# A two-layer relational graph network on one core: loads, x transposes and degree products of the front stage in another order

## The reference, cut to what matters

```python
# layer 0: degree of each node, counting the self loop; 1/sqrt(deg) on both ends of an edge
deg = segment_sum(ones, col, n); dinv = rsqrt(deg)
out = segment_sum((x @ W0)[row] * (dinv[row] * dinv[col])[:, None], col, n) + b0
x = layernorm(x + out)
# layer 1, twice (4 heads, then 1): per relation r
xr = einsum('nd,rdf->rnf', x, W); oi = xr[etype, dst]; oj = xr[etype, src]
alpha = leaky_relu(oi @ q + oj @ k); softmax over the edges with one dst
out = segment_sum(a * oj, dst, n) + b        # elu after the first
x = layernorm(x + layer1)
```

## Time and profile before

| | us |
|---|---|
| median of 3 runs | 1607.62 |
| lowest, highest | 1606.1, 1608.44 |
| the profiled execution | 1607.62 |
| its span | 1605.8 |

### The profile page before, as it was taken

The page is one execution under the profiler, slowest core; times in us unless marked ns, Lnnn a source line. Parts: engine busy times, 40 slices in busy tenths (PEclk is TensorE's granted clock), DMA queues, the critical chain, the costliest instruction groups (busy, mean ns, idle before and its releaser), DMA issues. The chain is left out here.

```text
span 1605.8 us, 23070 instructions
## 1 busy us (share of the span) xinstructions
PE 1396.8 (87%) x7239; PEld 1101.0 (69%) x7239; DVE 1135.7 (71%) x2394; ACT 401.6 (25%) x1013; POOL 385.4 (24%) x389
## 2 busy tenths in 40 slices
PE   6899978888888779999599999849998996999991
PEld 5566624554454479999599999828998993555550
DVE  9888887887776179995598888671554334666767
ACT  2222212233233111112244444352221210000003
POOL 1000000000000000000677777200000007777740
PEclk9799989999899889999799999959998997999996
DMA  6344301232232396662899998506664559999973
GB/s 223 138 158 157 137 3 52 81 99 71 80 104 70 120 328 204 206 178 76 311 328 318 321 328 300 135 4 202 189 191 135 189 163 312 323 322 318 319 221 96
DMA packets 105814, 301.51 MB, mean 188 GB/s; under 512 B 17677, under 2 KB 47183, under 8 KB 105663
## 3 DMA queue, kind: packets, MB, share of 16 engines
q1 hardware_dynamic: 77551, 160.68, 31.2%
q0 software_dynamic: 28160, 139.52, 25.6%
HBM read 245.31 MB, written 57.18 MB: 188 GB/s over the span
## 5 line engine op out<-in xcount | busy, mean ns | idle before, releaser
L1278 DVE CUSTOM_DVE_ANT_0 fl_early<-fl_masks,fl_gap 125x1250 bf16<-125x1250 f32 x120 | 166.8, 1465 | 23.6 <-DMA fl_masks<-fl_d_k 19.3
L815 PE MATMUL fr_ps<-fr_col_hot,fr_row_hot 125*128 x516 | 122.0, 368 | 50.0 <-DVE fr_col_hot L553 44.6
L1171 POOL DMA_INDIRECT xH<-fl_d_xr,edge_row x88 | 96.1, 1092 | 252.6 <-DMA fl_d_xr<-fl_xs 221.4
L1171 POOL DMA_INDIRECT xH<-sl_d_xr,edge_row x88 | 86.8, 987 | 270.9 <-DMA sl_d_xr<-sl_xs 240.8
L860 PE MATMUL fr_ps<-fr_h,fr_shared 125*125 125x384 f32 x400 | 142.1, 505 | 1.7 <-DVE fr_shared L581 1.7
L1549 PE MATMUL sl_ps<-xH,sl_hot 128*125 128x386 f32 x352 | 118.6, 495 | 17.6 <-DVE sl_hot L1352 17.5
L1509 PE MATMUL fl_ps<-fl_wH,xH 128*125 128x384 f32 x360 | 122.5, 340 | 9.6 <-ACT fl_xs L1192 9.6
L1228 ACT ACTIVATE fl_masks<-fl_plain,fl_ex 128x125 f32<-128x125 f32 x352 | 106.8, 385 | 93.8 <-PE fl_ps L1545 70.3
L1509 PE MATMUL sl_ps<-sl_wH,xH 128*125 128x384 f32 x360 | 124.7, 346 | 5.9 <-DVE sl_wL L1268 5.9
L1545 PE MATMUL fl_ps<-xH,fl_masks 128*125 128x194 f32 x704 | 121.5, 333 | 9.4 <-DVE fl_masks L1345 9.2
L1545 PEld LDWEIGHTS fl_ps<-xH,fl_masks 128*125 128x125 f32 x704 | 117.7, 190 | 10.4 <-issue 10.3
(11 more groups left out here) (269 smaller groups left out, 2530.4 us busy)
## 6 DMA issues: line engine op xcount, KB each, us to landing
fr_raw<-in_w SPq DMA_DIRECT2D x36, 384.0 KB, 3.7
fl_wH<-d_dl SPq DMA_DIRECT2D x22, 512.0 KB, 6.6
sl_before<-d_dl SPq DMA_DIRECT2D x22, 512.0 KB, 4.2
fl_d_xr<-fl_xs SPq DMA_DIRECT2D x60, 169.8 KB
sl_d_xr<-sl_xs SPq DMA_DIRECT2D x60, 168.9 KB
d_gap<-fr_gap SPq DMA_DIRECT2D x30, 312.5 KB, 2.5
fl_gap<-d_gap SPq DMA_DIRECT2D x30, 312.5 KB, 3.4
sl_before<-d_gap SPq DMA_DIRECT2D x30, 312.5 KB, 3.4
```

The costliest lines, as they stand in the source:

```text
L815: mm = pe.matmul(ps[:, par + h, 0:HC], row_hot[:, bass.ds(slot, 1), s, :].rearrange("p o n -> p (o n)"), col_hot[:, bass.ds(slot * TG + s, ...
L1171: pool.indirect_dma_start(rows(c // 4)[:, c % 4], None, d_xr, bass.IndirectOffsetOnAxis(ap=edge_row[:, c:c + 1], axis=0)).then_inc(gathere ...
L1278: v.tensor_tensor_reduce(dump[:, i % 2], krow[0:P, h * R + q % R], gap_all[0:P, q % GR], 1.0, -3e38, ALU.subtract, ALU.max, mk[:, q // R, ...
```

## The change

It puts instructions, waits and DMAs in another order and leaves their number and sizes as they are.

- SP: `step_dst` is loaded first, the copy of w0 before the six x tiles, and the x tiles 6 to 9 after q1 and k1.
- TensorE: all ten x tiles are turned first, then the sums and all ten batches of degrees; `transform(0)` goes before the transpose of the degrees.
- VectorE: the span group is first of all; `deg` is made after the positions, and `dinv` after the first batch of the list.

```diff
+            sp.dma_start(step_dst, dst.rearrange("(p n) -> p n", p=NG)).then_inc(dst_in, 16)
             for i, a in enumerate((src_t, dst_t, ety_t)):
                 sp.dma_start(ids[:, i, :], a).then_inc(ids_in, 16)
+            sp.dma_start(d_w0, w0).then_inc(w0_copied, 16)
             for e in range(RG):
                 load(e)
-            sp.dma_start(step_dst, dst.rearrange("(p n) -> p n", p=NG)).then_inc(dst_in, 16)
-            for e in range(RG, NT):
-                load(e)
-            sp.dma_start(d_w0, w0).then_inc(w0_copied, 16)
             sp.wait_ge(w0_copied, 16)
...
             for i, a in enumerate((q1, k1)):
                 sp.dma_start(qk1[:, :, i, :], a.rearrange("(c p) h -> p c h", p=CH),
                              allow_slow_non_contiguous=True).then_inc(qk1_in, 16)
+            for e in range(RG, NT):
+                load(e)
             sp.wait_ge(span_out, 32)
...
+            v.wait_ge(dst_in, 16)
+            link(v.tensor_copy(step_dstf, step_dst))
+            v.tensor_reduce(span[:, 0:1], step_dstf, AX.X, ALU.min).then_inc(span_made, 1)
+            v.tensor_reduce(span[:, 1:2], step_dstf, AX.X, ALU.max).then_inc(span_made, 1)
 
             v.wait_ge(lo_iota, 1)
...
             for b in range(ET // DB):
                 deg_hots(b)
-                if b == 1:
-                    v.wait_ge(dst_in, 16)
-                    link(v.tensor_copy(step_dstf, step_dst))
-                    v.tensor_reduce(span[:, 0:1], step_dstf, AX.X, ALU.min).then_inc(span_made, 1)
-                    v.tensor_reduce(span[:, 1:2], step_dstf, AX.X, ALU.max).then_inc(span_made, 1)
...
-            v.wait_ge(degT_turned, 1)
-            v.tensor_scalar(deg[:], ps[0:P, 7, 400:400 + NT], 1.0, None, ALU.add).then_inc(deg_made, 1)
             v.wait_ge(sums_done, 1)
...
-            v.wait_ge(root_deg, 1)
-            v.reciprocal(dinv[:], deg[:]).then_inc(dinv_made, 1)
...
+            v.wait_ge(degT_turned, 1)
+            v.tensor_scalar(deg[:], ps[0:P, 7, 400:400 + NT], 1.0, None, ALU.add).then_inc(deg_made, 1)
             for b in range(ET // LB):
                 list_hots(b)
-                if 1 <= b <= UNITS:
+                if b == 0:
+                    v.wait_ge(root_deg, 1)
+                    v.reciprocal(dinv[:], deg[:]).then_inc(dinv_made, 1)
+                elif b - 1 < UNITS:
                     split_low(b - 1)
...
             pe.wait_ge(ident_ready, 1)
-            for i in range(RG):
+            for i in range(NT):
                 turn_x(i)
+            pe.wait_ge(tile_hot_made, 1)
             pe.wait_ge(total_made, 1)
...
-            pe.wait_ge(tile_hot_made, 1)
             for b in range(ET // DB):
                 degrees(b)
-                if b % 2 and RG + b // 2 < NT:
-                    turn_x(RG + b // 2)
             pe.wait_ge(deg_used, ET // DB)
             pe.sem_inc(deg_done, 1)
-            pe.wait_ge(degT_copied, 1)
-            pe.transpose(ps[0:P, 7, 400:400 + NT], degT[:], ident[0:NT, 0:NT]).then_inc(degT_turned, 1)
             pe.wait_ge(x_copied, NT)
             pe.wait_ge(w0_in, 32)
             transform(0)
+            pe.wait_ge(degT_copied, 1)
             pe.wait_ge(base_made, 1)
+            pe.transpose(ps[0:P, 7, 400:400 + NT], degT[:], ident[0:NT, 0:NT]).then_inc(degT_turned, 1)
             transform(1)
```

## The result

| | before | after |
|---|---|---|
| median, us | 1607.34 (4 runs) | 1627.37 (4 runs) |
| ratio, 95% interval | | 1.0128 (1.0113 to 1.0142) |
| profiled execution, its span | 1607.62, 1605.8 | 1631.22, 1629.4 |

The record holds 15 executions of after, from 1623.39 to 1632.45 us, with a median of 1627.86; divided by 1607.34 that gives the ratio of 1.0128, while the two medians in the table alone give 1.0125. The profiled execution of after is 3.9 us above its median. Up to the last product of the list phase it is 20.6 us late, which is the loss of the medians (20.0); some 3 us more come in its later stages and are not in the medians.

A forecast was written before the change was run, and what follows sets the result against it. VectorE was taken to bound the kernel until 49 us, TensorE after about 59. Late tiles cost 14.6 us (not held) to 18.8 (held); the middle, 16.7, on 1607.6 gave 1624, range 1616 to 1630.

The forecast's parts named there:

- late tiles as summed: Main case: late x tiles delay VectorE's third degree one-hot by 14.6 to 18.8 us; 1620.5 to 1627 us, chance 0.66.
- part 4: SP queue: span stores may hold tiles 6 to 9 behind them; tile 6 at 28.0 us unheld, 30.3 held.
- Part 1: Head of VectorE: span group moved first costs 3.8 us, gains 1.0; the net 2.8 is hidden in the tile wait.
- Part 3: SP queue: w0 copy lands at 13.6 us, w0 data through at 23.8, tile 9 lands at about 30.8.
- the 6.5 us of the row: SP in the kernel before: span stores were in about 6.5 us after the last w0 data, taken as the full hold.
- Part 5: TensorE to VectorE: turning late tiles at half clock, sums and first degree batch put the third one-hot 14.6 to 18.8 us late.
- held case: Span stores hold tiles 6 to 9 for the full wait: third degree one-hot at 38.9 us, 18.8 late.
- Parts 6 and 7: VectorE's later deg and reciprocal, TensorE's transform 0 before the transpose of degrees: each counted as no gain, no loss.
- Sooner: Rival, DMA queue: tile 9 comes sooner, first degree batch done at 28.6 us, 8.4 late, 1616 us; chance 0.12.
- not slower: Rival, VectorE's third degree one-hot: loads hidden if the first degree batch ends by 23 us, down to 1606.6; chance 0.04.
- Held longer: Rival, SP queue: tile 6 issued only at 25 us, four tiles from 33 on, about 5 us more, 1630; chance 0.10.
- The kept clock: Rival, TensorE in list rounds 0 and 1: full clock saves 3.9 us, leaving 12.8 us late, 1620; chance 0.08.

The follow-up runs named there:

- e1: Changed kernel with the w0 copy and x tiles 6 to 9 back at their old places on SP: 1608.10 us, ratio 1.0005.
- e2: Changed kernel with x tiles 6 to 9 issued right behind the w0 loads, ahead of span stores, q1 and k1: 1616.67 us, ratio 1.0068.
- e3: Changed kernel with x tiles 6 to 9 between the span stores and the loads of q1 and k1: 1622.99 us, ratio 1.0101.
- e5: Kernel before with only SP's new load order, TensorE and VectorE orders unchanged: 1619.75 us, ratio 1.0071.
- e8: Changed kernel with the two span stores issued from ScalarE's DMA queue instead of SP's: 1624.38 us, ratio 1.0103.
- e10: Changed kernel with the span stored by one DMA of 80 8-byte pieces instead of two of 80 4-byte pieces: 1621.45 us, ratio 1.0078.
- e4: Changed kernel with the copy of w0 behind the first six x tiles instead of ahead of them: 1623.69 us, ratio 1.0100.

## Why the prediction was right, step by step

The forecast was 1624 us, the time is 1627.37, and the mechanism is the one that was named: tile 9's landing holds TensorE, TensorE holds VectorE's third degree one-hot, and the shift there is the shift of the end. The time lies inside the range of 1616 to 1630 and just above the narrower one (1620.5 to 1627) that the prediction gave for late tiles as summed. The chain is as it was drawn, but three of the places that it named came later than foretold: tile 9 at about 38 us (30 to 31), the first list one-hot at 69.39 (63 to 68), the last product at 212.03 (206 to 210); the idle time of VectorE (20.54 us, over 10) and the rounds of 14.07 us stand as said. All these misses go one way, and the term of part 4 makes most of them. The sizes:

- *Part 1, the span group.* `dst` was in at 2.73, not 4.5, and the ids cast ran at 5.96, not 8.7. The moved cast took 1.93 us instead of 0.28, and the two iota casts behind it 0.24 and 0.54 instead of 0.79 and 2.52. So this part cost 1.06 us against a gain of 0.97; all of it lay inside the wait, as said, and e1 shows the two cancel.
- *Part 3, the loads.* The copy was in at 12.22 (13.6), the w0 data through at about 23.5 (23.8). The working gave the copy 7.7 us of data in before, until 21.7 us. The slices of the earlier trace rows say less: 6.42 MB had moved by 19.5 us, which is all but 0.1 MB of the ids, x and the copy, so the data took some 5.5 us, and the landing at 23.67 came 4 us behind it. The sum of bytes ahead of tile 6 hides this slip.
- *Part 4, the price without a row.* This term was mis-sized. It was bounded by tile 6 at 28.0 and at 30.3; it came at 33.81, 3.5 us past the upper bound. The upper bound took a held completion, with the data already over when the stores landed. What the runs show is that the data waits as well, so its transfer comes on top: the stores were in at 31.8, 1.5 us past the 30.3, and tile 6 was ready 2.0 us later. The sign that the prediction named for a held landing, tiles 6 to 9 ready together, did not show, which says the same: this was more than a held landing. By e2 the stores and q1 and k1 together cost 9.0 us. That is above the 6.5 us of the row, since it includes q1 and k1 (3.4 us by e3).
- *Part 5, from landing to VectorE.* From tile 6 to the third one-hot it was 7.0 us, and 8.6 had been counted for the held case. The clock came back to full on the way (0.50 until 38 us, 1.00 from 39.4 us on): the two first degree batches together took 2.00 us, not 1.84 each. The prediction's value for the held case at full clock all through (16.4 us) does not come out of its own rows, which give about 15.5; the forecast did not use it.
- Held case in all: 38.9 predicted, + 3.5 (tile 6), - 1.6 (tail) = 40.8; measured 40.77. The forecast took the middle between held and not held, 2.1 us less than the held case, and that is the other half of the miss. The runs show neither of the two cases but a third, past the held one, so it is in part luck that their middle came within 3.4 us of the time.
- *Parts 6 and 7.* `deg` at 69.31 and the reciprocal at 74.30 stood where they were put. The second pair of transforms started at 84.66, 20.5 late like all else, so neither gained or lost.
- *The rivals.* Sooner, and not slower: no, tile 9 was turned at 39. Held longer: half true. Its four tiles from 33 us on are what came (33.81), and the time lies midway between its 1630 and the forecast, but not by its mechanism: SP issued tile 6 at 20.52 and not at 25, and the delay is the slow data. The kept clock: not in after, but in others. The second pair of transforms took 7.98 us in e2, e3, e5, e8 and e10, and 10.7 in e1 and e4. In these five the last product is 2.3 to 3.5 us less late than the first list one-hot (table). What sets it is open: e3 and e4 have nearly the same times until then, and one kept the clock.

This row of e2 shows such a pair, TensorE in order of time, against 10.75 in the earlier trace rows:

```profile
74.05 7.98 PE L763 MATMUL fr_ps<-xL,fr_C 128*125 128x384 f32 x24
```

## What to carry to other kernels

A load's place in the queue is a due time: before it is moved, find the engine whose in-order list reaches the consumer first, and count what stands behind that consumer there. The same late loads cost 12 us with the degree batches interleaved, 20 with all of them behind, and the new TensorE order alone cost nothing. Stores of a few bytes per row to DRAM should stand behind every load that someone waits for, and be merged into fewer stores and pieces; putting them on another queue did not help here, where they were issued at 5.46 us, ahead of most of the loads.

## What the runs showed of the hardware

- Two stores of 80 pieces of 4 bytes each, ahead of x tiles that moved at 400 GB/s without them (e2), brought the rate down to 37 to 155 GB/s for 7.5 us (e3), and with q1 and k1 (16-byte pieces) behind them to 12 to 55 GB/s for 7.5 us (after). From the other queue they left SP's loads 90 to 133 GB/s for 9 us (e8). One store of 80 pieces of 8 bytes, with q1 and k1 behind it, made a stall of about 3 us (e10); q1 and k1 without stores none (e8). The stall is invisible in before, where nothing stood behind them: there SP waited 9.5 us and no one else did.
- The same cast took very different times at different places: 80x250 int32 to f32 1.93 us at 2.73 (after), beside GpSimd's iotas and memsets, and 0.28 us at 19.23 (before), while GpSimd idled; 125x750 f32 to f16 2.52 us at 2.46 (before) and 0.54 us at 5.50 (after). GpSimd was not idle at 5.50 either: its own select (L388) ran from 5.00 on and took 1.52 us there, and 0.29 us in before. That the two engines slow each other, now one and now the other, fits these rows, but no run changed this alone, so it is not shown. These rows are of the kernel after:

```profile
2.73 1.93 DVE L475 CAST fr_shared<-fr_shared 80x250 f32<-80x250 int32 x1 [2.73 <-DMA fr_shared<-in_dst]
3.10 1.42 POOL L383 MEMSET fr_h<- 125x1600 bf16 x1
...
5.00 1.52 POOL L388 TENSOR_SCALAR_AFFINE_SELECT fr_tri<-fr_tri 125x125 f32<-125x125 f32 x1
...
5.50 0.54 DVE L483 CAST fr_io_col<-fr_shared 125x750 f16<-125x750 f32 x1
```
